# A split group's six f32r matmuls kept together, and a reordered front, in a recommendation tower with compressed interaction layers

## The chip, the cores and the metric

One core of a Trainium2 chip. The metric is the device time of one execution in microseconds (us). Engines: TensorE (PE; its weight loads are PEld), VectorE (DVE), ScalarE (ACT), GpSimd (POOL) and SyncE (SP), which only issues DMAs here.

## What is computed

39 embeddings of 16 numbers are looked up for each of 512 samples, go through a compressed interaction network of three layers, and then through a small dense tower.

```python
e = stack([tbl_f[ids[:, f]] for f in range(39)], axis=1)          # 512 x 39 x 16
x0 = xk = e
for idx, (W, b) in enumerate(((w0, b0), (w1, b1), (w2, b2))):     # 128 outputs each
    z = relu(einsum('bhd,bkd,hks->bsd', x0, xk, W) + b[None, :, None])
    if idx != 2:
        xk = z[:, :64, :]; direct.append(z[:, 64:, :])
    else:
        direct.append(z)
z = sum(concatenate(direct, axis=1), axis=-1)
h = relu(concatenate([z, dense_ctx], axis=1) @ W_top1 + b_top1)
h = relu(h @ W_top2 + b_top2)
y = h @ W_top3
```

All of it is float32.

## The kernel before

The batch is cut into 16 chunks of 32 samples; 32 samples x 16 numbers are the 512 columns of every matmul. Layers are called L0, L1, L2. A layer's sum over pairs (h, k) runs over groups g: each group is one product tile of two halves ("tiles", j = 0 and 1) of up to 128 rows by 512 columns, made by VectorE (lines 576, 595), and multiplied by weights of 128 columns on TensorE, all groups of a layer adding up in one PSUM tile, z0, z1 or z2. L0 has 4 groups (the last with one tile), L1 and L2 ten each.

**Whole and split groups.** A whole group is done with float32 matmuls from `prod` (sum_whole, line 685). The groups in SPLIT (line 45: one of L0, seven of L1, six of L2) are done in f32r: ScalarE rounds the product to `high` (line 433), GpSimd subtracts it from the product to get `low` (take_low, line 377), and TensorE does three matmuls a tile: high weights x high and low weights x high (sum_high, line 702), and high weights x low (sum_low, line 717). Four of these groups (THROUGH_PSUM, line 46) don't go by GpSimd: their product goes through the PSUM tile `base`, ScalarE rounds it (line 443), VectorE subtracts (line 638).

**Order on TensorE** (sum_stage, line 721). Group by group; where a group is split, its four matmuls on `high` are done in its place, and the two on `low` behind the next group. The waits are on `high_ready` ahead of the four and on `pool_low` ahead of the two (for the groups through PSUM on `tile_high` and `tile_low` for each tile).

**Order of the stages** (stages_of, line 64). Step i does L0 of chunk i, groups 0 to 5 of L2 of chunk i-1, L1 of chunk i, and groups 6 to 9 of L2 of chunk i-1 (in step 15: 0 to 3 and 4 to 9). Step 16 does L2 of chunk 15 alone. x1 is made from z0 by six ScalarE copies (line 453, relu0, placed behind L2's group 3), x2 from z1 by six more (relu1, ahead of the next chunk's L0 groups); VectorE's products of the next layer read them. For chunk 0 the x1 copies are shared: four by ScalarE (line 461) and four by VectorE (line 605).

**GpSimd** runs in one queue: chunk 0's and chunk 1's ten gathers (gather, line 367), then for each step the subtractions in the order of the groups, and behind some of them the gathers of chunk i+2 (FIRST_GATHERS for step 0, GATHERS_AFTER for all others, lines 48 and 50). Steps 14 and 15 have no gathers left.

**DMAs.** SP stores the gathered rows of a chunk twice to DRAM (store_x0, line 252), copies them there five more times (repeat_x0, line 265, `x0_copied`), loads `x0base` (line 281), the shifted copies `spread0` for L0 (lines 288 for chunk 0, 296 for the others) and the three pieces of `spread` for L1 and L2 (line 312). For chunk 0, `spread0` comes in three cuts (FIRST_CUTS), a third of each by ScalarE's queue (line 414). VectorE makes the low parts of the split weights ahead of all products (split_weights, line 644). The buffer rings: 8 slots of `prod`, 4 of `high` and `low`; a `high` slot is free when the split group four before is done on TensorE.

Of the kernel before, what the change touches and what calls it, by code (L numbers as in the profile page):

```python
# [8 lines left out]
P = 128  # L9
B = 512  # L10
F = 39
D = 16
# [127 lines left out]
def gathers_after(i, kind, g):  # L140
    return FIRST_GATHERS.get((kind, g), 0) if i == 0 else GATHERS_AFTER.get((kind, g), 0)

# [5 lines left out]
def tower_kernel(nc, ids, offsets, table, w0a, w0b, w1, w1_split, w2, w2_split, biases, wt1, bt1, wt2, bt2, wt3, ctxT, out):  # L148
    with ExitStack() as ctx:
# [101 lines left out]
        def _(sp):  # L251
            def store_x0(c):
# [4 lines left out]
                for at in (0, F):  # L257
# [142 lines left out]
        def _(act):  # L400
            def split_weights(kind, rows, w):
                act.activation(high_w[kind][0:rows, :, :].rearrange("p t s -> p (t s)"), w, ACT.Copy
                               ).then_inc(high_w_ready, 1)

            def load_first():

# [48 lines left out]

            def first_copies():

                act.wait_ge(mm_done, stage_end(0, "L0"))
                for tile in range(2):
                    for q in range(tile, FPT, 2):  # L460
                        act.activation(x1[q * QUAD:(q + 1) * QUAD, tile, :], z0[0:QUAD, :], ACT.Relu,
                                       bias=bias_sb[0:QUAD, 0:1]).then_inc(x1_ready, 1)

# [41 lines left out]
            split_weights("L2", P, w2_part)  # L505
            act.wait_ge(bias_in, 16)
            load_first()
            take_base(0)
            for i in range(NCH + 1):
# [5 lines left out]
                for c, kind, gs in stages_of(i):  # L515
                    for g in gs:
# [19 lines left out]
                    if kind == "L0" and i == 0:  # L536
                        first_copies()
                        relu0(i, 2)
# [15 lines left out]
        def _(dve):  # L554
# [25 lines left out]
            def wait_factors(c, kind, g):  # L580

                ready = x1_ready if kind == "L1" else x2_ready
                if g == 0:
                    dve.wait_ge(ready, (2 + FPT) * (c + 1) + (2 if kind == "L1" else 0))
                for p, (at, _) in enumerate(PIECES):
# [12 lines left out]

            def first_copies():

                dve.wait_ge(bias_in, 16)
                dve.wait_ge(mm_done, stage_end(0, "L0"))
                for tile in range(2):
                    for q in range(1 - tile, FPT, 2):
                        dve.tensor_scalar(x1[q * QUAD:(q + 1) * QUAD, tile, :], z0[QUAD:2 * QUAD, :],
                                          bias_sb[QUAD:2 * QUAD, 0:1], 0.0, ALU.add, ALU.max).then_inc(x1_ready, 1)

# [42 lines left out]
            dve.tensor_tensor(w0_all, w0_all, w0_mirror, ALU.add).then_inc(w0_folded, 1)  # L650
            split_weights("L0", R0, w0_sb[:, 2 * SPLIT["L0"][0]:2 * SPLIT["L0"][0] + 2, :].rearrange("p t s -> p (t s)"), 1)
            split_weights("L1", P, w1_part, 2)
            split_weights("L2", P, w2_part, 3)
            for i in range(NCH + 1):
                for c, kind, gs in stages_of(i):
# [16 lines left out]
                    if i == 0 and kind == "L0":  # L672
                        first_copies()
            sum2(NCH - 1)

        @block.tensor
        def _(pe):
            def sum_whole(c, kind, g, closes):

# [4 lines left out]
                for j in range(k):  # L684
                    last = pe.matmul(z[:, :], w[0:rows, at + j, :], prod[0:rows, slot(c, kind, g), j, :],  # L685
                                     start=g == 0 and j == 0, stop=closes and j == k - 1)
                last.then_inc(mm_done, 1)

            def sum_high(c, kind, g):

# [14 lines left out]
            def sum_low(c, kind, g, closes):  # L705

                z = {"L0": z0, "L1": z1, "L2": z2}[kind]
                at = 2 * SPLIT[kind].index(g)
                rows, k = shape_of(kind, g)
                h = split_slot(c, kind, g)  # L710
                tiled = TILED_NUMBER.get((c, kind, g))
                if not tiled:
                    pe.wait_ge(pool_low, POOL_NUMBER[c, kind, g])
                for j in range(k):
                    if tiled:
                        pe.wait_ge(tile_low, 2 * (tiled - 1) + j + 1)
                    last = pe.matmul(z[:, :], high_w[kind][0:rows, at + j, :], low[0:rows, h, j, :],  # L717
                                     start=False, stop=closes and j == k - 1)
                last.then_inc(mm_done, 1)

            def sum_stage(c, kind, gs):

                closing = stage_end(c, kind)
                if gs[0] == 0 and c >= 1:
                    pe.wait_ge({"L0": r0_ready, "L1": r1_ready, "L2": r2_ready}[kind], c)
                for g in gs:
                    if g in SPLIT[kind]:
                        sum_high(c, kind, g)
                    else:
                        sum_whole(c, kind, g, DONE[c, kind, g] == closing)  # L730
                    if g - 1 in gs and g - 1 in SPLIT[kind]:
                        sum_low(c, kind, g - 1, DONE[c, kind, g - 1] == closing)
                if gs[-1] in SPLIT[kind]:
                    sum_low(c, kind, gs[-1], DONE[c, kind, gs[-1]] == closing)

# [101 lines left out]
```

## Time and profile before

| | us |
|---|---|
| runs, median of 3 (lowest, highest) | 659.14 (658.57, 659.14) |
| the profiled execution, its own time | 658.7 |
| its span, first to last instruction | 656.9 |
| PE busy | 611.0 (93%) |
| PEld busy | 377.4 (57%) |
| DVE busy | 546.9 (83%) |
| ACT busy | 410.5 (62%) |
| POOL busy | 535.7 (82%) |
| mean granted clock of TensorE | 0.987 |

A row of the timeline gives the start, the time in us, the engine, the line, the operation and how many of them are merged (x4); in brackets the idle time of the engine before it and what ended it. Records of matmuls overlap, since they are pipelined, so the distance between starts tells what one takes. A float32 matmul leaves two records. "SPq" is the issuing of a DMA, not its transfer.

### The profile page before, as it was taken

What the parts mean: (1) busy time and instruction counts of PE and PEld (TensorE: products, weight loads), DVE (VectorE), ACT (ScalarE), POOL (GpSimd) and SP (SyncE); (2) the same over time, 40 slices, a digit from 0 to 9 for tenths busy, and PEclk for the clock granted to TensorE, in tenths of its full rate; (3) what the DMA queues carried; (4) which work ended last, traced back from release to release, by engine and by line L of the source; (5) the groups of instructions that cost most, each with busy time, mean ns of one, the idle gap of its engine ahead of it and who ended that gap; (6) DMA issues with size and microseconds to landing.
All of it is one profiled execution on the core that took longest, in us unless ns stands there. A gap on an engine that the chain in (4) does not pass through costs nothing.

```text
span 656.9 us, 6273 instructions
## 1 busy us (share of the span) xinstructions
PE 611.0 (93%) x1996; PEld 377.4 (57%) x1996; DVE 546.9 (83%) x616; ACT 410.5 (62%) x553; POOL 535.7 (82%) x325
## 2 busy tenths in 40 slices
PE   0069799999999999999999999999999999999998
PEld 0026466656666566666666665666566666655563
DVE  1268699998989898998989898989989898969740
ACT  2034758677666758576766757585777667575622
POOL 6758799898989899998989898999989886747520
PEclk9999799999999999999999999999999999999899
DMA  6597883838364645648373646557383735320000
GB/s 221 138 191 226 176 241 76 249 76 246 72 196 104 179 107 129 197 92 234 76 234 82 197 94 169 127 115 211 76 250 71 231 85 185 87 54 1 0 0 1
DMA packets 64044, 90.30 MB, mean 137 GB/s; under 512 B 46624, under 2 KB 49568, under 8 KB 60042
## 3 DMA queue, kind: packets, MB, share of 16 engines
q1 hardware_dynamic: 58682, 87.97, 49.7%
q0 software_dynamic: 5120, 1.29, 2.2%
q10 hardware_dynamic: 208, 0.64, 0.3%
q8 instruction: 16, 0.26, 0.2%
q14 instruction: 18, 0.15, 0.1%
HBM read 87.31 MB, written 8.95 MB: 147 GB/s over the span
## 4 chain that ended last, share of the span: by engine, by line
PE 38%; POOL 38%; ACT 11%; issue 6%; DMA 4%; DVE 3%; SPq 1%; DVEq 0%; ACTq 0%
POOL low L377 29%; PE z L685 20%; PE z L702 9%; POOL gat L367 9%; ACT x L453 7%; PE z L717 6%; ACT high L433 2%; DVE prod L595 2%; ACT r L477 1%; DMA x_rows<-gat 1%; DMA gat<-table_dram,index 1%; SPq L262 1%; DVE base L630 1%; DMA spread<-x_rows 1%; DVE low L638 1%
## 5 line engine op out<-in xcount | busy, mean ns | idle before, releaser
L377 POOL TENSOR_TENSOR low<-prod,high 128x1024 fp32r<-128x1024 f32 (+1 forms) x160 | 380.7, 2398 | 57.1 <-ACT high L433 55.9
L595 DVE TENSOR_TENSOR prod<-spread,x 128x1024 f32<-128x1024 f32 x256 | 308.1, 1214 | 38.4 <-ACT x L453 37.0
L685 PE MATMUL z<-prod,w_sb 128*128 128x512 f32 (+2 forms) x608 | 292.2, 601 | 36.5 <-DVE prod L576 31.9
L433 ACT ACTIVATE high<-prod 128x1024 fp32r<-128x1024 f32 (+1 forms) x160 | 167.7, 1058 | 119.5 <-DVE prod L595 98.8
L702 PE MATMUL z<-high,high_w_L 128*128 128x512 f32 (+1 forms) x448 | 205.0, 458 | 1.5 <-ACT high L443 1.0
L717 PE MATMUL z<-low,high_w_L 128*128 128x512 f32 (+1 forms) x448 | 182.4, 488 | 5.8 <-POOL low L377 4.4
L685 PEld LDWEIGHTS z<-prod,w_sb 128*128 128x128 f32 (+2 forms) x608 | 116.1, 192 | 122.5 <-issue 102.6
L367 POOL DMA_INDIRECT gat<-table_dram,index x160 | 154.4, 965 | 37.0 <-issue 35.2
L702 PE MATMUL z<-high,low_w_L 128*128 128x512 f32 (+1 forms) x448 | 179.4, 400 | 0.0
L453 ACT ACTIVATE x<-z,bias_sb 64x512 f32<-64x512 f32 (+1 forms) x186 | 120.2, 646 | 14.9 <-PE z L685 7.4
L717 PEld LDWEIGHTS z<-low,high_w_L 128*128 128x128 f32 (+1 forms) x448 | 82.7, 190 | 71.4 <-issue 45.2
L443 ACT ACTIVATE high<-base 128x512 fp32r<-128x512 f32 x128 | 75.5, 590 | 55.5 <-DVE base L630 55.0
L702 PEld LDWEIGHTS z<-high,high_w_L 128*128 128x128 f32 (+1 forms) x448 | 85.9, 192 | 39.2 <-issue 15.7
L702 PEld LDWEIGHTS z<-high,low_w_L 128*128 128x128 f32 (+1 forms) x448 | 85.8, 192 | 32.6 <-issue 14.8
L638 DVE TENSOR_TENSOR low<-base,high 128x512 fp32r<-128x512 f32 x128 | 87.7, 685 | 8.6 <-ACT high L443 8.3
L630 DVE TENSOR_TENSOR base<-spread,x 128x512 f32<-128x512 f32 x128 | 88.5, 692 | 2.2
L576 DVE TENSOR_TENSOR prod<-spread,base 117x1024 f32<-117x1024 f32 x64 | 65.4, 1082 | 17.9 <-DMA spread<-x_rows 15.4
L498 ACT ACTIVATE r<-z,bias_sb 128x512 f32<-128x512 f32 x16 | 11.0, 687 | 15.4 <-PE z L717 15.3
L616 DVE TENSOR_REDUCE logit<-r 128x32 f32<-128x512 f32 x16 | 10.9, 678 | 9.0 <-ACT r L498 9.0
L424 ACT ACTIVATE base<-x0base 117x512 f32<-117x512 f32 x16 | 9.6, 602 | 10.0 <-DMA x0base<-x_rows 9.7
L477 ACT ACTIVATE r<-z,bias_sb 64x512 f32<-64x512 f32 x16 | 11.0, 686 | 0.4
L491 ACT ACTIVATE r<-z,bias_sb 64x512 f32<-64x512 f32 x16 | 10.9, 683 | 0.4
(37 smaller groups left out, 61.1 us busy)
## 6 DMA issues: line engine op xcount, KB each, us to landing
spread<-x_rows SPq DMA_DIRECT2D x15, 1792.0 KB, 7.4
spread<-x_rows SPq DMA_DIRECT2D x32, 768.0 KB, 11.0
spread<-x_rows SPq DMA_DIRECT2D x16, 1024.0 KB, 7.5
x_rows<-x_rows SPq DMA_DIRECT2D x16, 390.0 KB
x0base<-x_rows SPq DMA_DIRECT2D x47, 78.0 KB
gat<-table_dram,index POOLq DMA_INDIRECT x160, 3.6
x_rows<-gat SPq DMA_DIRECT2D x32, 72.0 KB, 2.3
wt_sb<-wt_dram SPq DMA_DIRECT2D x2, 512.0 KB, 17.6
```

Of the source, the lines that this page charges most:

```text
L367: pool.indirect_dma_start(out=gat[0:rows, c % GBUF, j, :], out_offset=None, in_=table, in_offset=bass.IndirectOffsetOnAxis(ap=index[0:rows ...
L377: pool.tensor_tensor(low[0:rows, h, 0:k, :], prod[0:rows, slot(c, kind, g), 0:k, :], high[0:rows, h, 0:k, :].bitcast(F32), ALU.subtract).t ...
L433: act.activation(high[0:rows, split_slot(c, kind, g), 0:k, :], prod[0:rows, slot(c, kind, g), 0:k, :], ACT.Copy).then_inc(high_ready, 1)
L443: act.activation(high[0:rows, split_slot(c, kind, g), t, :], base[0:rows, :], ACT.Copy).then_inc(tile_high, 1)
L453: act.activation(to[at:end, tile, :], z[k:k + end - at, :], ACT.Relu, bias=bias_sb[k:k + end - at, layer:layer + 1]).then_inc(ready, 1)
L576: dve.tensor_tensor(prod[0:rows, slot(c, "L0", g), 0:k, :], spread0[0:rows, 2 * g:2 * g + k, :], base[0:rows, :].unsqueeze(1).to_broadcast ...
L595: dve.tensor_tensor(prod[0:rows, slot(c, kind, g), :, :], spread[0:rows, c % 2, g, :].unsqueeze(1).to_broadcast([rows, k, N]), x[0:rows, : ...
L630: dve.tensor_tensor(base[0:rows, :], spread[0:rows, c % 2, g, :], x[0:rows, t, :], ALU.mult).then_inc(tile_prod, 1)
L638: dve.tensor_tensor(low[0:rows, h, t, :], base[0:rows, :], high[0:rows, h, t, :].bitcast(F32), ALU.subtract).then_inc(tile_low, 1)
L685: last = pe.matmul(z[:, :], w[0:rows, at + j, :], prod[0:rows, slot(c, kind, g), j, :], start=g == 0 and j == 0, stop=closes and j == k - 1)
L702: pe.matmul(z[:, :], v[kind][0:rows, at + j, :], high[0:rows, h, j, :], start=g == 0 and j == 0 and v is high_w, stop=False)
L717: last = pe.matmul(z[:, :], high_w[kind][0:rows, at + j, :], low[0:rows, h, j, :], start=False, stop=closes and j == k - 1)
```

## The change

It has these parts.

- sum_high and sum_low become one function, sum_split. It is called behind the next group, where sum_low was. For each tile: low weights x high, high weights x high, then high weights x low. The wait on `pool_low` stands behind the first tile's first two matmuls, that on `tile_low` behind each tile's first two. The start flag goes to the group that is done first.
- Front on SP and ScalarE: ScalarE's queue stores the second copy of chunk 0's rows; SP issues repeat_x0(0) behind all three cuts.
- VectorE waits for chunk 0's gathers before the low parts of L1's and L2's split weights.
- x2 of chunk 0 is copied by ScalarE (four) and VectorE (four), as x1 was.
- Three gathers behind L1's group 9 in step 0 become one each behind L1's groups 2, 5 and 9; the two gathers of step 1 behind L0's group 0 go behind its group 1.

```diff
-FIRST_GATHERS = {("L0", 1): 7, ("L1", 9): 3}
+FIRST_GATHERS = {("L0", 1): 7, ("L1", 2): 1, ("L1", 5): 1, ("L1", 9): 1}
+SECOND_GATHERS = {("L0", 1): 2, ("L2", 1): 3, ("L1", 2): 1, ("L1", 4): 1, ("L1", 8): 1, ("L2", 6): 2}
 GATHERS_AFTER = {("L0", 0): 2, ("L2", 1): 3, ("L1", 2): 1, ("L1", 4): 1, ("L1", 8): 1, ("L2", 6): 2}
...
-            store_x0(0)
+            store_x0(0, (0,))
             load_base(0, (0, 1))
             for n, (at, end) in enumerate(FIRST_CUTS):
                 load_first(at, end, spread0_first[n], (0, 1))
-                if n == 0:
-                    repeat_x0(0)
+            repeat_x0(0)
...
+            def store_first_again():
+
+                act.wait_ge(gathered[0], 16 * GAT)
+                first = x0_dram[0, F:F + 1, 0:1]
+                act.dma_start(bass.AP(first.tensor, first.offset, [[D, P], [FPT * N, GAT - 1], [1, D]]),
+                              gat[:, 0, 0:GAT - 1, :]).then_inc(x0_stored[0], 16)
...
             act.wait_ge(bias_in, 16)
+            store_first_again()
             load_first()
...
                         if i == 1 and kind == "L0" and g == 1:
-                            for part in range(3):
-                                relu1(0, part)
+                            first_copies(x2, z1, "L1", 1, x2_ready)
+                            relu1(0, 2)
...
+            dve.wait_ge(gathered[0], 16 * GAT)
             split_weights("L1", P, w1_part, 2)
             split_weights("L2", P, w2_part, 3)
...
+                    if i == 1 and kind == "L0":
+                        first_copies(x2, z1, "L1", 1, x2_ready)
...
-            def sum_high(c, kind, g):
+            def sum_split(c, kind, g, starts, closes):
...
                 for j in range(k):
                     if tiled:
                         pe.wait_ge(tile_high, 2 * (tiled - 1) + j + 1)
-                    for v in (high_w, low_w):
-                        pe.matmul(z[:, :], v[kind][0:rows, at + j, :], high[0:rows, h, j, :],
-                                  start=g == 0 and j == 0 and v is high_w, stop=False)
...
+                    pe.matmul(z[:, :], low_w[kind][0:rows, at + j, :], high[0:rows, h, j, :],
+                              start=starts and j == 0, stop=False)
+                    pe.matmul(z[:, :], high_w[kind][0:rows, at + j, :], high[0:rows, h, j, :],
+                              start=False, stop=False)
                     if tiled:
                         pe.wait_ge(tile_low, 2 * (tiled - 1) + j + 1)
+                    elif j == 0:
+                        pe.wait_ge(pool_low, POOL_NUMBER[c, kind, g])
                     last = pe.matmul(z[:, :], high_w[kind][0:rows, at + j, :], low[0:rows, h, j, :],
                                      start=False, stop=closes and j == k - 1)
...
                 for g in gs:
-                    if g in SPLIT[kind]:
-                        sum_high(c, kind, g)
-                    else:
-                        sum_whole(c, kind, g, DONE[c, kind, g] == closing)
+                    if g not in SPLIT[kind]:
+                        sum_whole(c, kind, g, g == opening, DONE[c, kind, g] == closing)
                     if g - 1 in gs and g - 1 in SPLIT[kind]:
-                        sum_low(c, kind, g - 1, DONE[c, kind, g - 1] == closing)
+                        sum_split(c, kind, g - 1, g - 1 == opening, DONE[c, kind, g - 1] == closing)
```

## Rows read from the trace of the kernel before

**Rows 1.** The page: busy times with instructions, and the chain that ended last.

```profile
PE 611.0 (93%) x1996; PEld 377.4 (57%) x1996; DVE 546.9 (83%) x616; ACT 410.5 (62%) x553; POOL 535.7 (82%) x325
...
PE 38%; POOL 38%; ACT 11%; issue 6%; DMA 4%; DVE 3%; SPq 1%; DVEq 0%; ACTq 0%
```

**Rows 2.** Windows: one chunk's period; stretch, its length, busy us of each engine.

```profile
172.30:208.70 36.40, 36.25 (x123) 22.84 (x123) 33.69 (x39) 25.14 (x35) 33.36 (x20) 1.00 0.56 148
```

**Rows 3.** The chain in order of time, 278 to 318 us: start, us, what.

```profile
278.88 2.42 POOL low L377
...
281.34 0.74 PE z L717 x2
282.08 0.93 PE z L702 x4
283.01 1.72 PE z L685 x4
...
294.02 0.65 ACT x L453
...
299.91 4.72 POOL low L377 x2
...
315.21 2.41 POOL low L377
```

**Rows 4.** Timeline at the end of L1 of one chunk, 317 to 319 us.

```profile
317.67 0.30 PEld L717 LDWEIGHTS z<-low,high_w_L 128*128 128x128 f32 x2 [0.55 <-POOL low L377]
317.67 0.73 PE L717 MATMUL z<-low,high_w_L 128*128 128x512 f32 x2
...
318.01 0.19 PEld L702 LDWEIGHTS z<-high,high_w_L 128*128 128x128 f32 x1
318.23 0.40 PE L702 MATMUL z<-high,high_w_L 128*128 128x512 f32 x1
...
318.43 0.65 ACT L453 ACTIVATE x<-z,bias_sb 64x512 f32<-64x512 f32 x1 [0.18 <-PE z L717]
```

**Rows 5.** Timeline of the front, 14 to 46 us, then one piece of the chain.

```profile
14.05 0.95 POOL L367 DMA_INDIRECT gat<-table_dram,index  x1 [0.30 <-issue]
15.25 3.69 DVE L644 TENSOR_TENSOR low_w_L<-spread,high_w_L 128x1792 fp32r<-128x1792 f32 x2 [6.51 <-ACT high_w_L L402]
15.30 2.77 POOL L367 DMA_INDIRECT gat<-table_dram,index  x1 [0.30 <-issue]
...
19.37 0.38 SPq L259 DMA_DIRECT2D x_rows<-gat  x1
...
20.44 0.43 SPq L259 DMA_DIRECT2D x_rows<-gat  x1
...
24.92 0.92 SPq L270 DMA_DIRECT2D x_rows<-x_rows  x1
...
30.55 1.22 DVE L576 TENSOR_TENSOR prod<-spread,base 117x1024 f32<-117x1024 f32 x1 [11.61 <-DMA spread<-x_rows]
...
36.76 1.82 DVE L576 TENSOR_TENSOR prod<-spread,base 117x1024 f32<-117x1024 f32 x2 [1.78 <-DMA spread<-x_rows]
...
38.03 2.80 PE L685 MATMUL z<-prod,w_sb 117*128 117x512 f32 x4
...
45.43 2.35 DVE L595 TENSOR_TENSOR prod<-spread,x 128x1024 f32<-128x1024 f32 x2
...
51.07 3.70 DMA x_rows<-x_rows
```

**Rows 6.** Line 312, chunk 0's second and third piece (issued 33.0 and 33.6).

```profile
DMA to landing us min/median/max: 10.3/12.2/14.2
```

**Rows 7.** Timeline, x1 copies of chunk 0 and step 1, 42 to 72 us.

```profile
42.27 3.12 DVE L605 TENSOR_SCALAR x<-z,bias_sb 32x512 f32<-32x512 f32 x4 [3.70 <-PE z L685]
...
61.89 4.08 DVE L576 TENSOR_TENSOR prod<-spread,base 117x1024 f32<-117x1024 f32 x4 [2.15 <-ACT base L424]
...
69.25 2.35 DVE L595 TENSOR_TENSOR prod<-spread,x 128x1024 f32<-128x1024 f32 x2 [3.29 <-ACT x L453]
...
71.82 1.22 PE L717 MATMUL z<-low,high_w_L 117*128 117x512 f32 x2 [3.39 <-POOL low L377]
```

More of the change, by code:

```diff
@@ L140, in gathers_after @@
 def gathers_after(i, kind, g):
-    return FIRST_GATHERS.get((kind, g), 0) if i == 0 else GATHERS_AFTER.get((kind, g), 0)
+    return (FIRST_GATHERS if i == 0 else SECOND_GATHERS if i == 1 else GATHERS_AFTER).get((kind, g), 0)
 def stage_end(c, kind):
@@ L251, in _, with store_x0 @@
         def _(sp):
-            def store_x0(c):
+            def store_x0(c, copies=(0, 1)):
                 sp.wait_ge(gathered[c % GBUF], 16 * GAT * (c // GBUF + 1))
@@ L256, in store_x0 @@
                 full = GAT - 1
-                for at in (0, F):
+                for n in copies:
+                    at = n * F
                     first = x0_dram[c, at:at + 1, 0:1]
@@ L454, in copies, with first_copies @@
                                    bias=bias_sb[k:k + end - at, layer:layer + 1]).then_inc(ready, 1)
-            def first_copies():
-                act.wait_ge(mm_done, stage_end(0, "L0"))
+            def first_copies(to, z, kind, layer, ready):
+                act.wait_ge(mm_done, stage_end(0, kind))
                 for tile in range(2):
                     for q in range(tile, FPT, 2):
-                        act.activation(x1[q * QUAD:(q + 1) * QUAD, tile, :], z0[0:QUAD, :], ACT.Relu,
-                                       bias=bias_sb[0:QUAD, 0:1]).then_inc(x1_ready, 1)
+                        act.activation(to[q * QUAD:(q + 1) * QUAD, tile, :], z[0:QUAD, :], ACT.Relu,
+                                       bias=bias_sb[0:QUAD, layer:layer + 1]).then_inc(ready, 1)
             def relu0(c, part):
@@ L583, in wait_factors @@
                 if g == 0:
-                    dve.wait_ge(ready, (2 + FPT) * (c + 1) + (2 if kind == "L1" else 0))
+                    dve.wait_ge(ready, (2 + FPT) * (c + 1) + 2)
                 for p, (at, _) in enumerate(PIECES):
@@ L597, in product, with first_copies @@
                                   x[0:rows, :, :], ALU.mult).then_inc(prod_done, 1)
-            def first_copies():
-                dve.wait_ge(bias_in, 16)
-                dve.wait_ge(mm_done, stage_end(0, "L0"))
+            def first_copies(to, z, kind, layer, ready):
+                dve.wait_ge(mm_done, stage_end(0, kind))
                 for tile in range(2):
                     for q in range(1 - tile, FPT, 2):
-                        dve.tensor_scalar(x1[q * QUAD:(q + 1) * QUAD, tile, :], z0[QUAD:2 * QUAD, :],
-                                          bias_sb[QUAD:2 * QUAD, 0:1], 0.0, ALU.add, ALU.max).then_inc(x1_ready, 1)
+                        dve.tensor_scalar(to[q * QUAD:(q + 1) * QUAD, tile, :], z[QUAD:2 * QUAD, :],
+                                          bias_sb[QUAD:2 * QUAD, layer:layer + 1], 0.0, ALU.add, ALU.max
+                                          ).then_inc(ready, 1)
             def sum01(c):
@@ L672, in _ @@
                     if i == 0 and kind == "L0":
-                        first_copies()
+                        dve.wait_ge(bias_in, 16)
+                        first_copies(x1, z0, "L0", 0, x1_ready)
+                    if i == 1 and kind == "L0":
+                        first_copies(x2, z1, "L1", 1, x2_ready)
             sum2(NCH - 1)
@@ L677, in _, with sum_whole @@
         def _(pe):
-            def sum_whole(c, kind, g, closes):
+            def sum_whole(c, kind, g, starts, closes):
                 z, w = {"L0": (z0, w0_sb), "L1": (z1, w1_sb), "L2": (z2, w2_sb)}[kind]
@@ L685, in sum_whole @@
                     last = pe.matmul(z[:, :], w[0:rows, at + j, :], prod[0:rows, slot(c, kind, g), j, :],
-                                     start=g == 0 and j == 0, stop=closes and j == k - 1)
+                                     start=starts and j == 0, stop=closes and j == k - 1)
                 last.then_inc(mm_done, 1)
-            def sum_high(c, kind, g):
+            def sum_split(c, kind, g, starts, closes):
                 z = {"L0": z0, "L1": z1, "L2": z2}[kind]
@@ L700, in sum_high @@
                         pe.wait_ge(tile_high, 2 * (tiled - 1) + j + 1)
-                    for v in (high_w, low_w):
-                        pe.matmul(z[:, :], v[kind][0:rows, at + j, :], high[0:rows, h, j, :],
-                                  start=g == 0 and j == 0 and v is high_w, stop=False)
[L705 to L714, printed above, removed]
+                    pe.matmul(z[:, :], low_w[kind][0:rows, at + j, :], high[0:rows, h, j, :],
+                              start=starts and j == 0, stop=False)
+                    pe.matmul(z[:, :], high_w[kind][0:rows, at + j, :], high[0:rows, h, j, :],
+                              start=False, stop=False)
                     if tiled:
                         pe.wait_ge(tile_low, 2 * (tiled - 1) + j + 1)
+                    elif j == 0:
+                        pe.wait_ge(pool_low, POOL_NUMBER[c, kind, g])
                     last = pe.matmul(z[:, :], high_w[kind][0:rows, at + j, :], low[0:rows, h, j, :],
@@ L726, in sum_stage @@
                 for g in gs:
-                    if g in SPLIT[kind]:
-                        sum_high(c, kind, g)
-                    else:
-                        sum_whole(c, kind, g, DONE[c, kind, g] == closing)
+                    if g not in SPLIT[kind]:
+                        sum_whole(c, kind, g, g == opening, DONE[c, kind, g] == closing)
                     if g - 1 in gs and g - 1 in SPLIT[kind]:
-                        sum_low(c, kind, g - 1, DONE[c, kind, g - 1] == closing)
+                        sum_split(c, kind, g - 1, g - 1 == opening, DONE[c, kind, g - 1] == closing)
                 if gs[-1] in SPLIT[kind]:
-                    sum_low(c, kind, gs[-1], DONE[c, kind, gs[-1]] == closing)
+                    sum_split(c, kind, gs[-1], gs[-1] == opening, DONE[c, kind, gs[-1]] == closing)
             pe.wait_ge(w1_in, 32)
```

6 lines of the change are left out of this document (5 added, 1 removed).

## The prediction

> **What bounds the kernel now.** First the share of the chain of work that ended last [rows 1]: PE and POOL hold 38% each, ACT 11%. So it is no plain TensorE kernel, though in one chunk's period TensorE is recorded busy 36.25 of 36.40 us and GpSimd 33.36 [rows 2]. Then the same chain in order of time over one chunk [rows 3]. The reader is to see a closed loop. At 281.30 the last GpSimd subtraction of a chunk's L1 stage ends (278.88 + 2.42); TensorE does its two low matmuls, then the rest of L2 and all of L0, until ScalarE copies x1 at 294.02; at 299.91 GpSimd starts its run of six subtractions with three gathers between them, back to back until 317.62 (315.21 + 2.41). One turn is 315.21 - 278.88 = 36.33 us. In parts: 0.05 to TensorE, 12.68 on TensorE until the copies (281.34 to 294.02), 5.89 of copies and rounding (to 299.91), 17.71 of GpSimd. These add up to 36.33: no slack in the loop. TensorE, nearly full, has some: before the subtraction that closes the stage it waits 0.55 us [rows 4]. A f32r matmul takes 0.93 / 4 = 0.233 us, a whole group of two float32 matmuls 1.72 [rows 3].
>
> **The order of the matmuls.** No matmul goes or comes. A split group has six f32r matmuls, 1.40 us. Before, four (on `high`) came ahead of the wait for `low` and two behind it. Now, in a GpSimd group, the wait stands behind the first tile's two; four are behind it: low of tile 0 and all three of tile 1. Where GpSimd is the last to arrive, as at 317.67, TensorE has 2 x 0.233 = 0.47 us more to do after it. After the change: the restart (318.01 less 317.67 = 0.34, then the rest 0.22, so the next group began at 318.23 [rows 4]) and 0.47, z1 complete at 318.70.
> Does TensorE get there in time, so that this counts in full? A walk from the end of L0 (z0 complete at 293.83, 0.19 ahead of the copies): L2's split 0 and 1, whole 3, split 2, whole 4 take 3 x 1.40 + 2 x 1.72 = 7.63, plus two matmuls 0.47: 301.93. The `low` it then needs is the first of the run at 299.91 (4.72 for two, so 302.27): a new wait of 0.4 us. Likewise L1's split 5 gets there about 311.3, and its `low`, fourth in the run behind two gathers, ends at 299.91 + 4 x 2.39 + 2 x 1.13 = 311.7 (a gather with its issue is (17.71 - 6 x 2.39) / 3). From there 0.93 + 1.40 + 1.72 + 1.40 + 0.47 = 5.92 brings TensorE to 317.6, level with 317.62. So these waits add up to the time that TensorE had to spare and little more, and none is on the loop; what is, is the 0.47 at its end. Nothing gives it back: between z1 complete and z0 complete the same groups run as before (L2 6 to 9, L0 0 to 3), and their `low` halves, for which TensorE had no wait, are needed only 0.47 us sooner (two matmuls stand ahead of the wait instead of four). Behind the blocked TensorE queue stand only its own later groups; VectorE's buffers and the `high` slots come free no later, since a split group completes at the same place or up to 0.9 us sooner.
> Loop: 36.33 + 0.47 = 36.8. It turns 13 times (chunks 1 to 13): +6.1. Chunks 14 and 15 have no gathers, TensorE or VectorE leads; there the new wait in L2's split 5 costs 0.4 and that behind L1's split 1 about 0.3. **Together +6.8.** Lower bound: nothing, if it were all hidden; upper: both new waits on the path too, 0.9 a chunk, +12; I take 0.47 because the loop's own rows close to 0.01 us.
> **Same weights side by side.** Loads take 377.4 us beside the matmuls, as many loads as matmuls, 1996 [rows 1]. 0.233 is above the 0.215 of one pass of a float32 group (1.72 / 8), so a load that needn't be made could be worth 0.018. No row has two matmuls in a row on the same weights: a saving of 0 to 0.018 on 28 pairs a chunk, of which six lie between z1 and z0 and two behind the last `low`. I take 0, since the source still gives each matmul its own weights and every row of it shows a load.
> The Trainium skill (TensorE: Matmul & The Clock Gate, "Step-by-step: what each phase is for") says that a load apart from the compute lets one load serve several matmuls. By it the pair would share a load; the second rival is what that would give. No run here shows it yet.
>
> **The front.** (a) VectorE's two weight splits from 15.25 wait for the gathers. The tenth gather took 2.77 beside them, its neighbour 0.95: -1.8 [rows 5]. They move onto chunk 1's gathers, which lose there what chunk 0's win and so end where they did; the splits end near 21.5, ahead of the first matmul (30.55 + 1.2). (b) The second copy of x0 goes to ScalarE's queue: a pair of stores occupies SP for 20.44 - 19.37: -1.1 (ScalarE is idle there). (c) The repeat goes behind all cuts: SP reaches the later cuts 0.92 sooner (its own issue time at 24.92), and its traffic, 3.70 alone at 51.07, leaves their way. For the last product that waits on a cut (36.76) that is -0.9 to -3.7; I take -2.6, nearer the upper end, since the repeat stood ahead of these cuts in SP's own queue while ScalarE's queue had its share too. The first product (30.55) gains (a) and (b) only. (d) Against it: L0's split group now does six matmuls behind the group 2 of chunk 0 instead of two. Four groups' records took 2.80 at 38.03 instead of 1.72, so the clock was still rising: 4 x 0.233 x 1.6 = +1.5 (bounds 0.9 and 1.9). x1 is ready -1.8 - 1.1 - 2.6 + 1.5 = 4.0 sooner, 41.4 instead of 45.43 [rows 5]. (e) Cover: the pieces of `spread` now start behind the later repeat. The third landed 14.2 after 33.6, at 47.8 [rows 6], and is first used some 8 us behind x1 ready, at 49.7: 1.9 to spare, the first two alike. But chunk 1's own stores stand in SP's queue behind them, and their repeat (51.07) and spread0 follow; if these don't move, VectorE's first group of chunk 1 can't start the full 4.0 sooner. I take 0.3 off.
> (f) x2's copies shared: the page of the changed kernel should show them, but VectorE is busy to 65.97 (61.89 + 4.08) and four such copies took 3.12 (42.27), so it ends at 69.1 where the products started at 69.25 [rows 7]: -0.15, taken as 0 to 0.2. (g) Fewer gathers ahead of L0's subtraction in chunk 1: TensorE's 3.39 us idle before 71.82 goes, and is replaced by a wait for L2's products, which start from the x2 copies. Worth nothing: the x1 copies of chunk 1 hang on VectorE's products from 69.25, not on TensorE. The gathers put among L1 of chunk 0 fall in GpSimd's idle gaps.
> **Front: -3.7** (bounds: -1 if spread or the stores are late, -6 if (c) gives all and (d) least).
>
> **Sum.** +6.8 - 3.7 = +3.1. The profiled execution was 658.7 (span 656.9, 1.8 around it), the median of the runs is 659.1: 661.8 for a profile, **662.2** for a median. A measurement can tell about 0.2%, 1.3 us.
>
> **Rivals.**
> 1. The loop doesn't lengthen and TensorE's waits vanish, because nothing is needed early: the period falls towards TensorE's own work, 84 x 0.233 + 9.5 x 1.72 = 35.9, -0.45 in 13 chunks, with the front -3.7: **649.5**. For it: TensorE is the fullest engine and its 0.55 wait [rows 4] goes. Against: the loop holds 17.7 us of GpSimd that no edit shortens. Decides if the chain at z1's end doesn't name a subtraction. 0.08.
> 2. A shared load. The loop gains 8 x 0.018 = 0.14 and the restart behind `low` up to 0.1 more: +0.23 a chunk instead of 0.47, so +3.3 - 3.7: **658.7**. 0.10.
> 3. The front gives little: `spread` or chunk 1's stores come as late as before; -1, **665**. Sign of it: VectorE waiting for a DMA before an L1 product or before the L0 products of chunk 1. 0.15.
> 4. The front gives all, -6: **660**. 0.10.
> The forecast itself has 0.57. A front that helps and a loop that costs pull in opposite directions; what is slower here is one mechanism, the two matmuls behind the closing `low`, from the point where GpSimd arrives within 0.5 us of TensorE.
>
> **Numbers.** Slower by over 0.2% takes in the forecast's bulk (662.2 give or take 1.5: nine tenths), rival 3, and half of 4: 0.71. Within 0.2%: rival 2, the rest of these: 0.17. Faster: rival 1 and the tails: 0.12. Range 657.0 to 666.0: it leaves out rival 1 and the far tails of the others.
>
> **What would show it.** Right: the closing subtraction to the x2 copies goes from 0.82 us (317.62 to the copies at 318.43) to about 1.3; the chunk's period from 36.33 to 36.8; TensorE's wait for GpSimd rises by about 0.4 a chunk at L2's split 5; as many loads as matmuls still there; the first L1 product near 41.5 to 42. Wrong: an unchanged period, fewer loads, a spacing of 0.215 in the pairs, or a front that saves over 6.

## The result and the profile after

The changed kernel takes 666.74 us (median of 4 runs, 665.9 to 667.1) beside 658.95 for the kernel before on the same chip: a ratio of 1.0134, with an interval of 1.0107 to 1.016. It is slower, as forecast, but by 7.8 us where 3.1 were forecast, and outside the range. The profiled execution took 666.61 us, its span 664.5 (before 656.9), its mean granted clock 0.987 as before.

The page of the changed kernel answers to [rows 1].

```profile
PE 614.6 (92%) x1996; PEld 375.9 (57%) x1996; DVE 550.1 (83%) x620; ACT 410.9 (62%) x551; POOL 537.1 (81%) x325
...
PE 51%; POOL 25%; ACT 11%; issue 4%; DMA 4%; SPq 2%; DVE 2%; ACTq 0%
```

No matmul and no load went. In the chain GpSimd gave 13 points to TensorE, so the loop closes in another place. Three rows date it: in the timeline of GpSimd the first subtraction of a chunk's run of six (L2's group 5), here for chunks 1, 7 and 14.

```profile
83.25 4.74 POOL L378 TENSOR_TENSOR low<-prod,high 128x1024 fp32r<-128x1024 f32 x2 [1.96 <-ACT high L444]
...
304.28 4.74 POOL L378 TENSOR_TENSOR low<-prod,high 128x1024 fp32r<-128x1024 f32 x2 [1.22 <-ACT high L444]
...
562.24 7.09 POOL L378 TENSOR_TENSOR low<-prod,high 128x1024 fp32r<-128x1024 f32 x3 [4.85 <-ACT high L444]
```

Before, the same three stood at 81.79, 299.91 and 554.32. That splits the 7.6 us of span:

| stretch | forecast | measured |
|---|---|---|
| front, to GpSimd's run in chunk 1 | -3.7 | 83.25 - 81.79 = +1.46 |
| 13 turns of the loop | +6.1 | 478.99 - 472.53 = +6.46 (0.50 each) |
| chunks 14 and 15, to the x1 copies of 15 | +0.7 | (592.77 - 562.24) - (584.36 - 554.32) = +0.49 |
| the rest | 0 | 71.73 - 72.54 = -0.81 |

**The loop.** The chain in order of time answers to [rows 3].

```profile
304.28 4.74 POOL low L378 x2
...
313.72 2.42 POOL low L378
...
316.18 0.50 PE z L725
...
323.05 0.23 PE z L725
323.28 1.72 PE z L701 x4
```

Before, the chain stayed on GpSimd to the sixth subtraction (`low` of L1's group 9) and crossed to TensorE there. Now it crosses after the fourth (group 5, done at 316.14), and from 316.18 TensorE never pauses until z1 is complete at 323.28. The timeline of TensorE, GpSimd and ScalarE around that (answering to [rows 4]) shows how close the two places are.

```profile
316.18 0.50 PE L725 MATMUL z<-low,high_w_L 128*128 128x512 f32 x1 [0.18 <-POOL low L378]
...
316.74 0.40 PE L719 MATMUL z<-high,high_w_L 128*128 128x512 f32 x1
316.98 0.40 PE L725 MATMUL z<-low,high_w_L 128*128 128x512 f32 x1
...
319.63 2.41 POOL L378 TENSOR_TENSOR low<-prod,high 128x1024 fp32r<-128x1024 f32 x1
...
322.19 0.41 PE L725 MATMUL z<-low,high_w_L 128*128 128x512 f32 x1
...
323.32 4.01 ACT L464 ACTIVATE x<-z,bias_sb 64x512 f32<-64x512 f32 x6 [0.70 <-PE z L725]
```

The last subtraction ends at 319.63 + 2.41 = 322.04, and the matmul that needs it starts at 322.19 with no idle time in front. From the end of that subtraction to the x2 copies are 1.28 us (forecast 1.3; before 0.82). The pair on the same weights, L719 and L725, starts 0.23 apart like the others (316.74, 316.98).

**The front.** VectorE and SP in the timeline, answering to [rows 5, 7].

```profile
29.13 1.22 DVE L588 TENSOR_TENSOR prod<-spread,base 117x1024 f32<-117x1024 f32 x1 [6.96 <-DMA spread<-x_rows]
...
33.89 1.82 DVE L588 TENSOR_TENSOR prod<-spread,base 117x1024 f32<-117x1024 f32 x2 [1.02 <-DMA spread<-x_rows]
35.17 3.78 PE L701 MATMUL z<-prod,w_sb 117*128 117x512 f32 x4 [0.92 <-DVE prod L588]
37.96 1.42 PE L717 MATMUL z<-high,low_w_L 117*128 117x512 f32 x1
...
45.08 2.35 DVE L607 TENSOR_TENSOR prod<-spread,x 128x1024 f32<-128x1024 f32 x2
...
63.31 4.08 DVE L588 TENSOR_TENSOR prod<-spread,base 117x1024 f32<-117x1024 f32 x4 [3.94 <-issue]
```

The last L0 product of chunk 0 comes 2.87 us sooner (33.89 for 36.76), but the first L1 product only 0.35 (45.08 for 45.43), and the L0 products of chunk 1 come 1.42 later (63.31 for 61.89), with VectorE idle for 3.94 us before them. What they wait for stands in the chain of the same stretch.

```profile
26.03 8.91 DMA x_rows<-x_rows
...
34.96 0.60 SPq L314
...
36.88 0.90 SPq L261
...
37.83 6.12 SPq L264
...
44.58 6.54 DMA x_rows<-gat
...
51.13 0.31 SPq L283
```

The pieces of `spread` (L314) wait for the repeat to land, at 34.94 (26.03 + 8.91). Chunk 1's stores stand behind them in SP's queue, from 36.88, and are on DRAM at 51.12 (44.58 + 6.54); `x0base`, the repeat and `spread0` follow, and 12 us later the products. The same view of the kernel before, a part that the prediction had not read:

```profile
30.07 6.92 DMA gat<-table_dram,index
...
37.00 0.40 SPq L259
...
37.44 4.69 SPq L262
...
42.67 7.21 DMA x_rows<-gat
...
49.89 0.31 SPq L281
```

There the stores began with the landing of chunk 1's gathers and took 12.9 us (37.00 to 49.89); now they begin level with that, and take 14.3 (36.88 to 51.13).

### The profile page after: what moved, and what is told of

Its sections match the earlier page's. It is cut to its first block, busy times and chain, and to the rows that moved or that the text cites. A ratio compares the mean times of both kernels' runs of the same rounds, so it can differ in the third digit from the quotient of the medians.

```text
span 664.5 us, 6276 instructions
## 1 busy us (share of the span) xinstructions
PE 614.6 (92%) x1996; PEld 375.9 (57%) x1996; DVE 550.1 (83%) x620; ACT 410.9 (62%) x551; POOL 537.1 (81%) x325
## 4 chain that ended last, share of the span: by engine, by line
PE 51%; POOL 25%; ACT 11%; issue 4%; DMA 4%; SPq 2%; DVE 2%; ACTq 0%
PE z L701 23%; POOL low L378 20%; PE z L725 9%; PE z L719 8%; PE z L717 8%; ACT x L464 6%; POOL gat L368 5%; ACT high L444 3%; DMA x_rows<-x_rows 2%; ACT r L488 1%; DMA x_rows<-gat 1%; SPq L264 1%; DVE prod L607 1%; DVE prod L588 1%; PE base L769 1%
## 5 line engine op out<-in xcount | busy, mean ns | idle before, releaser
L717 PE MATMUL z<-high,low_w_L 128*128 128x512 f32 (+1 forms) x448 | 236.5, 528 | 1.6 <-ACT high L444 1.6
L725 PE MATMUL z<-low,high_w_L 128*128 128x512 f32 (+1 forms) x448 | 182.5, 407 | 9.5 <-POOL low L378 9.0
L719 PE MATMUL z<-high,high_w_L 128*128 128x512 f32 (+1 forms) x448 | 178.6, 399 | 0.0
L464 ACT ACTIVATE x<-z,bias_sb 64x512 f32<-64x512 f32 (+1 forms) x180 | 116.3, 646 | 21.5 <-PE z L725 9.3
L719 PEld LDWEIGHTS z<-high,high_w_L 128*128 128x128 f32 (+1 forms) x448 | 85.5, 191 | 48.2 <-issue 34.3
L725 PEld LDWEIGHTS z<-low,high_w_L 128*128 128x128 f32 (+1 forms) x448 | 85.0, 190 | 45.8 <-POOL low L378 26.7
L656 DVE TENSOR_TENSOR low_w_L<-spread,high_w_L 128x1792 fp32r<-128x1792 f32 (+1 forms) x2 | 3.7, 1888 | 10.1 <-DMA gat<-table_dram,index 10.1
L616 DVE TENSOR_SCALAR x<-z,bias_sb 32x512 f32<-32x512 f32 x8 | 6.1, 757 | 6.4 <-PE z L701 6.2
## 6 DMA issues: line engine op xcount, KB each, us to landing
spread<-x_rows SPq DMA_DIRECT2D x32, 768.0 KB, 10.7
```

Source lines behind the costliest of these rows:

```text
L464: act.activation(to[at:end, tile, :], z[k:k + end - at, :], ACT.Relu, bias=bias_sb[k:k + end - at, layer:layer + 1]).then_inc(ready, 1)
L717: pe.matmul(z[:, :], low_w[kind][0:rows, at + j, :], high[0:rows, h, j, :], start=starts and j == 0, stop=False)
L719: pe.matmul(z[:, :], high_w[kind][0:rows, at + j, :], high[0:rows, h, j, :], start=False, stop=False)
```

## The experiments

First the order of the matmuls and the front are taken apart, then each is narrowed down. Each ratio is against the kernel before, run beside it on the same chip.

**The order alone.** The kernel before with only the change of sum_split:

```diff
-            def sum_high(c, kind, g):
...
-            def sum_low(c, kind, g, closes):
+            def sum_split(c, kind, g, starts, closes):
```

> The kernel before with the new order of the matmuls alone; no other edit. Loop theory (two more matmuls behind the subtraction that closes L1's stage): a chunk's period of 36.8 us instead of 36.33, 13 times, and 0.7 in the last two chunks: about +7, 666. If the cost of the change lay in its front, this kernel would be at 659 to 660.

667.14 us, ratio 1.0148 (1.0097 to 1.0199): as slow as the whole change. The period of GpSimd's run is 36.85 (156.92 to 193.77). In the front too the order costs: from the last L0 product of chunk 0 to the first L1 product 11.47 us (35.33 to 46.80) where the kernel before takes 8.67 (36.76 to 45.43).

**The front alone.** The changed kernel with sum_high and sum_low restored.

```diff
-            def sum_split(c, kind, g, starts, closes):
+            def sum_high(c, kind, g):
...
+            def sum_low(c, kind, g, closes):
```

> The changed kernel with the order of the matmuls of before; all of the new front stays. Loop theory: period back to 36.33. The front: its cuts are in 2.9 us sooner, but SP's chain (repeat behind the cuts, pieces of spread, chunk 1's stores and repeat, spread0) is 1.25 later and x2's copies end 1.3 later, so the run of subtractions of chunk 1 starts 1 to 1.5 later than before: 660 to 660.5. If the front helps on its own and lost only by the slow clock behind it: 656 to 658.

658.04 us, ratio 1.0008 (0.9986 to 1.0031): no difference, neither the gain that the prediction gave the front (3.7 us, or 5.2 without the cost of the order in it) nor the loss of 1 to 1.5 expected here. The period is 36.33. The first L1 product stands at 41.56, the full 3.9 sooner, and then VectorE waits for DMAs; its chain shows where it went.

```profile
24.42 9.24 DMA x_rows<-x_rows
...
35.60 0.82 SPq L261
...
43.41 6.70 DMA x_rows<-gat
...
50.13 0.31 SPq L283
...
62.10 0.31 DVE prod L588
```

62.10 is 0.2 later than before: the four us gained for chunk 0 come to nothing at chunk 1's first products.

**Four matmuls ahead of the wait.** The changed kernel, with its whole groups later, but all four matmuls on `high` ahead of the wait:

```diff
+                if not tiled:
+                    pe.wait_ge(pool_low, POOL_NUMBER[c, kind, g])
+                for j in range(k):
                     if tiled:
                         pe.wait_ge(tile_low, 2 * (tiled - 1) + j + 1)
-                    elif j == 0:
-                        pe.wait_ge(pool_low, POOL_NUMBER[c, kind, g])
```

> The changed kernel, split groups still one group later, but all four matmuls on high ahead of the wait for low, two behind it. Loop theory: only what stands behind the wait counts, so the period goes back to 36.3 to 36.4 and the time to 660 to 661. Rival (doing a split group one group later is what costs): period stays at 36.8, time at 666 to 667.

658.0 us, ratio 1.0011 (0.9987 to 1.0035), period 36.35. So not the place of the group costs, nor its being done as a whole, but what stands behind the wait.

**The same weights apart.** The changed kernel with the first two matmuls of a tile exchanged, so that no two neighbours share weights:

```diff
-                    pe.matmul(z[:, :], low_w[kind][0:rows, at + j, :], high[0:rows, h, j, :],
-                              start=starts and j == 0, stop=False)
                     pe.matmul(z[:, :], high_w[kind][0:rows, at + j, :], high[0:rows, h, j, :],
+                              start=starts and j == 0, stop=False)
+                    pe.matmul(z[:, :], low_w[kind][0:rows, at + j, :], high[0:rows, h, j, :],
```

> The changed kernel with the first two matmuls of each tile swapped, so that no two matmuls side by side have the same weights. If such a pair saves nothing: the same as the changed kernel, 666.7, with matmuls 0.233 us apart. If a shared load saved up to 0.018 a pair, 1 to 4 us slower than it.

665.78 us, ratio 1.0141 (1.009 to 1.0193), period 36.85 (155.68 to 192.53), the same as with the pair. The pairing is worth nothing that can be seen.

**All six behind the wait.** The order alone, with the wait ahead of all six:

```diff
-                    pe.wait_ge(high_ready, POOL_NUMBER[c, kind, g])
+                    pe.wait_ge(pool_low, POOL_NUMBER[c, kind, g])
...
-                    elif j == 0:
-                        pe.wait_ge(pool_low, POOL_NUMBER[c, kind, g])
```

> e1_order with the wait for GpSimd's low ahead of all six matmuls of a split group (four of the groups go by VectorE and keep their waits). Loop theory: four matmuls more than before stand behind the closing subtraction instead of two, so the period grows by 0.93 us over 36.34 to 37.3, twice the growth of e1_order, and the time is 7 above e1_order's: 672 to 674. If only the number of new waits or the one group's delay mattered: as e1_order, 666 to 667.

676.4 us, ratio 1.0282 (1.0251 to 1.0313). Two starts of GpSimd's run in its timeline:

```profile
308.96 4.73 POOL L377 TENSOR_TENSOR low<-prod,high 128x1024 fp32r<-128x1024 f32 x2 [1.27 <-ACT high L433]
...
346.24 2.37 POOL L377 TENSOR_TENSOR low<-prod,high 128x1024 fp32r<-128x1024 f32 x1 [1.26 <-ACT high L433]
```

The period is 37.28: 36.34, 36.85, 37.28 with two, four and six matmuls behind the wait. Each step of two matmuls, 0.47 us by the spacing, costs 0.51 and 0.43. The time itself came 2 to 4 us above what was expected; the front, where the run of chunk 1 stands at 85.21, holds that.

**Only the closing group.** Is it the closing group's wait that counts, as the prediction says, or the one behind group 5? The changed kernel with four ahead and two behind for L1's group 9 alone:

```diff
+                if closes and kind == "L1":
+                    for j in range(k):
+                        for v in (low_w, high_w):
+                            pe.matmul(z[:, :], v[kind][0:rows, at + j, :], high[0:rows, h, j, :],
+                                      start=False, stop=False)
+                    pe.wait_ge(pool_low, POOL_NUMBER[c, kind, g])
+                    for j in range(k):
+                        last = pe.matmul(z[:, :], high_w[kind][0:rows, at + j, :], low[0:rows, h, j, :],
+                                         start=False, stop=j == k - 1)
...
```

> The changed kernel, but L1's closing group 9 alone does its four matmuls on high ahead of the wait for low and two behind it; the twelve other split groups keep the new order. The prediction's mechanism says that the 0.47 us stand at the closing group's wait: the period of a chunk falls from 36.85 back to 36.4, the time to about 660. The rival, read from the chain of the changed kernel: the wait that counts is the one behind L1's group 5, which the low of the fourth place in GpSimd's run ends and behind which TensorE never pauses again until z1 is complete; the same six matmuls of the closing group are then done in another order and nothing is gained: period 36.85 (36.8 to 36.9), time 665 to 667. In between (36.55 to 36.7) it would be both.

665.37 us, ratio 1.0119 (1.01 to 1.0138), period 36.83. The rival holds. Its chain:

```profile
303.08 4.73 POOL low L378 x2
...
312.49 2.43 POOL low L378
...
314.96 0.50 PE z L736
...
321.61 0.47 PE z L721 x2
322.07 1.72 PE z L701 x4
```

Line 721 is the closing group's last pair; TensorE came to it without a pause from 314.96, and z1 is complete 18.99 us behind the start of the run (322.07 - 303.08), as in the changed kernel (323.28 - 304.28 = 19.00). With the closing wait eased, the wait behind group 5 alone gives the whole period. The counterpart, with that wait eased and the closing one kept, was not run.

**A smaller loop.** If matmuls behind GpSimd's `low` lengthen the loop, matmuls moved ahead of the wait should shorten it. In the kernel before, L1's closing pair goes behind the four matmuls on `high` of L2's group 6, which need no `low`; so four matmuls (0.93 us) come ahead of the wait that stood behind it:

```diff
+            held = []
...
+                    if held:
+                        sum_low(*held.pop())
...
-                    sum_low(c, kind, gs[-1], DONE[c, kind, gs[-1]] == closing)
+                    late = (c, kind, gs[-1], DONE[c, kind, gs[-1]] == closing)
+                    if keep:
+                        held.append(late)
+                    else:
+                        sum_low(*late)
...
-                    sum_stage(c, kind, gs)
+                    sum_stage(c, kind, gs, kind == "L1" and 1 <= i < NCH - 1)
```

> The kernel before, with the two low matmuls that close L1 done behind the four high matmuls of L2's group 6 (those need nothing late), in chunks 1 to 14. Loop theory: 0.93 us of TensorE's work moves out of the stretch behind the closing subtraction into the wait ahead of it; the period falls from 36.34 to what TensorE's own 35.9 and the later x2 copies allow, 35.9 to 36.1: 3 to 6 us less than before. If the loop is not what sets the period: no change, or slower by the later z1 (0.65 us a chunk, +8).

651.63 us, ratio 0.9907 (0.9879 to 0.9936): faster than both kernels. One period in the windows view, and the chain's shares on the page:

```profile
152.35:188.31 35.96, 35.96 (x123) 22.89 (x123) 33.65 (x39) 25.12 (x34) 33.35 (x20) 1.00 0.57 149
...
PE 85%; POOL 5%; DMA 4%; DVE 2%; issue 2%; SPq 1%; ACT 1%; DVEq 0%
```

TensorE is busy 35.96 of 35.96 us [rows 2 had 36.25 of 36.40]: the loop is gone, and TensorE's own work, put at 35.9 in the first rival, bounds the chunk.

**Chunk 1's stores on ScalarE's queue.** The front alone, with chunk 1's four stores issued by ScalarE behind its rounding of L0's group 1:

```diff
-            store_x0(1)
...
+                        if i == 0 and (kind, g) == ("L0", 1):
+                            store_second()
```

> e2_front with chunk 1's four stores on ScalarE's queue, behind its rounding of L0's group 1, instead of in SP's queue behind chunk 0's pieces of spread. Theory (the chain of chunk 1's stores, repeat and spread0 on SP's queue holds VectorE back 6.2 us ahead of chunk 1's first product, 62.10): that product starts 3 to 5 us sooner and nearly all of it shows: 653 to 655, against 658 for e2_front. If something else holds it (x0base, ScalarE): within 1 us of e2_front.

657.77 us, ratio 0.9989 (0.997 to 1.0008); a miss. ScalarE's timeline says why:

```profile
36.23 5.69 ACTq L423 DMA_DIRECT2D x_rows<-gat  x1
41.97 2.65 ACT L482 ACTIVATE x<-z,bias_sb 32x512 f32<-32x512 f32 x4 [8.62 <-issue]
```

The issue of the second small store holds ScalarE for 5.69 us, and its x1 copies come behind it: first L1 product 44.65 instead of 41.56.

With the stores out of SP's queue VectorE's L0 products of chunk 1 start at 60.68, only 1.4 sooner, and now right behind ScalarE's `base` instead of a DMA. GpSimd's run of chunk 1 starts at 80.61, 1.4 sooner too; but the next one starts at 118.24. In this turn of 37.63 us TensorE's granted clock was 0.95 in the mean: 0.50, the lower of its two levels (1.2 GHz), from 84 to 87 us, and 1.00 again behind 88. In the run with the repeat back, below, GpSimd's run starts level at 80.62, the clock stays at 1.00, and the next one starts at 116.94, 36.32 later. So in this profiled execution the fall of the clock took back 1.3 us. TensorE's pauses ahead of 84 us are the same in both (0.72 and 1.26 here, 0.73 and 1.26 there), so why the clock fell is open, and so is how often it does.

**Both of these together.**

```diff
-            store_x0(1)
...
+                    if held:
+                        sum_low(*held.pop())
```

> k2_front_stores and k1_carry together. The first acts ahead of chunk 1, the second on the 13 turns: the gains add, 649 to 651.

653.92 us, ratio 0.9941 (0.9915 to 0.9967): a miss too, no better than the smaller loop alone.

**The repeat back behind the first cut.** The front alone, without that one move:

```diff
+                if n == 0:
+                    repeat_x0(0)
-            repeat_x0(0)
```

> e2_front (new front, old order of matmuls) with chunk 0's repeat back behind the first cut. Theory (SP's chain of repeat, pieces, stores and spread0 sets chunk 1's first product, and TensorE's own work takes over behind it): that product moves from 62.1 to 59.5 to 61, the run of subtractions of chunk 1 from 82.0 to 80 to 81; the time changes by less than 1.5 us against e2_front, 656.5 to 658, since behind chunk 1 TensorE has no idle time to give. If the place of the repeat were what the front loses by: 2 us or more below e2_front, 654 to 656.

655.7 us, ratio 0.996 (0.9939 to 0.9981): below what the theory then held gave, and inside the rival's 654 to 656. Its chain:

```profile
30.80 8.04 DMA gat<-table_dram,index
...
38.86 0.40 SPq L261
...
39.30 1.54 SPq L264
...
41.36 7.42 DMA x_rows<-gat
...
48.79 0.31 SPq L283
```

Chunk 1's stores take 9.9 us here (38.86 to 48.79) instead of 14.5 (35.60 to 50.13 in the front alone); its L0 products start at 60.69, 1.4 sooner than with the move, GpSimd's run at 80.62. The 1.4 us last to GpSimd's final subtraction (628.97 for 630.42). So by these two runs, made on two chips, the rest of the front is a gain of a few tenths of a per cent, and moving the repeat takes it back; the two intervals (0.9939 to 0.9981, and 0.9986 to 1.0031) only just stay apart, and the spans of the two profiled executions don't differ (653.9 and 653.8), since what comes behind the last subtraction took 1.5 us more here.

**The smaller loop with that front.** The edit of the smaller loop and the front with the repeat back, together:

```diff
+                if n == 0:
+                    repeat_x0(0)
...
+                    if held:
+                        sum_low(*held.pop())
```

> k1_carry with the front of e7_repeat_back. With the closing low matmuls put off, TensorE's own work is the period, so a front can only bring what it takes from TensorE's idle time ahead of chunk 2. If the front helps: 649 to 650.5. If it doesn't, as in k3_both against k1_carry: 651 to 654.

652.52 us, ratio 0.9898 (0.9872 to 0.9923), period 35.97. And the smaller loop once more, beside it on the same chip, with the same edit as above:

```diff
-                    sum_stage(c, kind, gs)
+                    sum_stage(c, kind, gs, kind == "L1" and 1 <= i < NCH - 1)
```

> k1_carry once more, on the same chip as k4_carry_front for the comparison: 651 to 652, period 35.97.

653.89 us, ratio 0.9927 (0.9898 to 0.9955). The two intervals overlap: the smaller loop is worth 0.7 to 0.9 per cent, and that this front adds to it is not settled.

## Why the prediction was right and wrong

**The loop was right in size, wrong in place.** Forecast 0.47 a turn, measured 0.50; 36.8 and 36.85. The two walks of TensorE came out level at the closing subtraction, and the prediction then said that of the new waits "none is on the loop; what is, is the 0.47 at its end". The run on the closing group alone disproves the first half: with the 0.47 at the end taken away the period stays. The wait behind group 5 is on the loop: the last `low` ends at 322.04 and TensorE arrives at 322.19, a little behind it, not ahead. The second half is not disproved. By the closing `low` alone the next group would start at 322.04 + 0.05 + 0.56 + 0.47 = 323.12 (an estimate, with the restart of [rows 4]: 317.62 to 317.67, and to 318.23), and in the timeline it does start at 323.12 (the chain, which ends a step 0.16 later, has 323.28).

That both paths give the same number is luck. Behind the wait for group 5's `low` stood 16 f32r matmuls and a whole group until z1 before, and 22 and a whole group after: not two but six more, 1.40 us. Before, this path would have had z1 complete at about 311.73 + 0.15 + 16 x 0.233 + 1.72 = 317.33 (an estimate: group 5's `low` ended at 309.32 + 2.41, and 0.15 is a restart), 0.9 ahead of the 318.23 where it was; 1.40 less 0.9 is 0.5. The first four of the six cost nothing: the run with four ahead has 20 there and a period of 36.35. The last two are what the runs vary: from the start of GpSimd's run to z1 complete are 18.5 us with two matmuls behind the wait (320.06 - 301.55 in the run with four ahead), 19.0 with four, 19.44 with six (328.40 - 308.96).

**Same weights side by side: right, 0.** The Trainium skill (TensorE: Matmul & The Clock Gate, "Step-by-step: what each phase is for") says that one load can serve several matmuls; here the page shows 1996 loads for 1996 matmuls, and exchanging the pair left the period at 36.85. The rule needs loads that aren't issued, and this source issues one for each matmul. Rival 2 falls.

**The front was wrong: -3.7 forecast, +1.5 measured.** By its steps:
- (a) As forecast for the gather (0.93 us at 16.09 where it took 2.77), but the first store comes 0.90 sooner (18.47 for 19.37), not 1.8: the third gather took 1.65 us where it had taken 0.94. And it isn't a gain of the change in each execution: with the old code the tenth gather took 0.92 and 0.93 in two other profiles, 1.68 and 2.48 in two more. In the kernel before, the gather started 0.05 behind VectorE's splits (15.30, 15.25) and took 2.77; started 0.01 ahead of them or 0.02 behind it took 0.92 and 0.93. The Trainium skill (SBUF — State Buffer, "Who interferes with whom") says that VectorE with two SBUF inputs and GpSimd reading SBUF exclude each other; by it the outcome hangs on who is first, and the rows agree to within their 0.02. The third gather agrees too: it started 0.26 behind VectorE's addition of two SBUF tiles (6.63, 6.37), and 0.17 ahead of it before (6.56, 6.73). VectorE's later products, which take one input from PSUM, leave a gather at 0.94 us (298.19, within the product from 298.06 of the kernel before).
- (b) 1.1 forecast, 0.4 measured: from the first store to `x0base` are 3.58 us (18.47 to 22.05) instead of 3.95 (19.37 to 23.32). `x0base` waits for the stores to land (3.05 us in the chain), not for SP's issuing.
- (c) From the first to the last L0 product of chunk 0 are 4.76 us instead of 6.21, and 3.9 to 4.5 in four other profiles with this front: 1.5 to 2.3 sooner, where 2.6 were taken.
- (d) 1.5 forecast, 2.5 read from these two profiles: 11.19 us from the last L0 product to the first L1 product instead of 8.67. Matmuls still stood 0.43 apart (starts at 39.17, 39.60, 40.03) when all six came behind group 2; before, four were done ahead of it, while TensorE had nothing else. The profile's granted clock of 33 to 40 us is 1.00 in both, so the rising clock that the prediction read from such spacings isn't shown by it; the spacings are. The step varies between executions: with this order it was 10.7 to 11.5 in three other profiles and 9.27 in a fourth (the same weights apart), with the old order 8.0 to 9.5 in five others.
- (e) This is the step that failed. "I take 0.3 off" for chunk 1's stores; in truth they take all. Its L0 products start 12 us behind `x0base` of chunk 1: 61.89 - 49.89 = 12.00 before, 63.31 - 51.13 = 12.18 after, 62.10 - 50.13 = 11.97 with the front alone. In the four other runs in which VectorE stands idle ahead of them for over 3 us it is 11.6 to 12.4. So 61.89 was already held by the DMAs of chunk 1, 0.4 behind the compute (ScalarE's `base` was done at 60.85 + 0.61 = 61.46), and nothing gained in chunk 0 could pass them. That chain starts from GpSimd's twenty gathers, which end where they did, as step (a) itself said. Worse, (c) loaded it: the repeat lands at 34.94, the pieces start at 34.96 instead of 32.33, and their traffic lies beside chunk 1's stores, which take 14.3 us instead of 12.9. In all profiles with the moved repeat they take 13.7 to 14.5, in all others with these stores on SP's queue 9.9 to 13.3. That the repeat's place does it is shown by the run with the repeat back; that it works through the pieces' traffic is read from the order of the rows, not shown by itself.
- (f), (g) Right, nothing: the x2 products start 7.27 us behind chunk 1's L0 products (70.58 - 63.31), before 7.36 (69.25 - 61.89). From those L0 products to GpSimd's run are 19.9 us in both.

So rival 3, with its sign (VectorE waiting for a DMA before the L0 products of chunk 1), was the case, and it went past its own size: it counted on the DMAs coming "as late as before", and they came later.

**Chunks 14 and 15** cost 0.5 where 0.7 were forecast. **The rest**, the end of L2 and the dense tower, gave 0.8 back, which was not forecast: the granted clock of the last 75 us was 0.98 after and 0.96 before. No effect of the order shows in it. To the last subtraction 0.42 are lost (46.44 - 46.02), and from there to the end 1.23 gained (25.29 - 26.52); in the twelve other profiles that last stretch takes 23.4 to 26.6 us, with the new order (25.0 to 26.6) as with the old (23.4 to 26.5).

## What to carry to other kernels

In a closed loop over engines, count what stands behind each wait for the loop's slowest engine, and put work that doesn't need it ahead: two more matmuls behind the wait, with the group one place later, cost 1.3%, and four others ahead of it won 0.7 to 0.9%. Where two paths come out level to a tenth of a us, don't name one of them; the experiment on one alone tells. And before a gain in a front is booked, follow every chain into the next stage: a start that two chains hold to within half a us can't be moved by one.

## What was not expected of the hardware

- A store of the last few rows (line 262 before, 264 after, 423 on ScalarE's queue) is issued in 0.58 to 0.80 us when little is under way. Chunk 1's two such stores, behind other stores, pieces and gathers, held SP's queue for 3.9 to 6.4 us each (once 1.54), and the second of them ScalarE's for 5.69 and 6.65: a queue that also computes stands still with it.
- The granted clock can fall for a few us in the middle of work that keeps it at 1.00 in another execution: 0.50 from 84 to 87 us in the run with chunk 1's stores on ScalarE's queue, 1.00 there with the repeat back. It took 1.3 us.
- The front's start varies by 2.5 us between executions of the same code (first L0 product at 28.73 to 31.24 with the old front), in part by which of VectorE's split and GpSimd's tenth gather comes first.
